# A decoder layer's cross-attention: VectorE turns the maxima, row transfers in four pieces, two loads merged, two sums moved

## Chip, core and metric

The kernel runs on one NeuronCore of one Trainium2 chip. Times are device microseconds (us) of that core. The median of three runs of the kernel before is 801.43 us (801.19 to 803.54).

## The reference

```python
x = x + attn(layernorm(x))             # 32 heads of 16, causal, grouped keys; x is (4, 512, 512)
x = x + xattn(layernorm(x), ctx, ctx)  # ctx (4, 512, 512) is both keys and values
x = x + ffn(layernorm(x))              # three ternary-weight matmuls, activations rounded to 8 bits

def xattn(q, k, v):                    # (b, 512, 512) each, 8 heads of 64 rows: 32 heads in all
    qk = einsum('bdm,bdn->bmn', qh, kh) * 64 ** -0.5
    sm = softmax(qk, axis=-1)
    return einsum('bmn,bcn->bcm', sm, vh)

def ffn(x):                            # qlinear rounds x per row: scale = max|x| / 127 + eps
    return qlinear(silu(qlinear(x, w_gate)) * qlinear(x, w_up), w_down)
```

The scores of the cross-attention decide a sharp softmax, so the kernel computes them from a high and a low part of queries and keys.

## The kernel before

All engines run programs written out by hand and meet through semaphores. The function `rest_of_layer` holds the part that the change touches: attention output (steps 0 to 18), cross-attention (steps `i` of `attend_context`, 3 to 43) and feed-forward bodies (`feed(i)`). The last eight steps of the cross-attention, 36 to 43, alternate with feed-forward bodies 2 to 9.

The 32 heads are taken as 16 pairs, one head on partitions 0 to 63 and one on 64 to 127. `pair_due(i, k)` says which pair has a piece of work in step `i`, `k` steps after its first; each piece comes every second step. For pair p, in order of time:

- **First scores** (L1597): steps 2p+1 and 2p+2, four 128x512 blocks each, into the banks `p1`, three in turn. VectorE takes each block's maximum over 512 queries' scores into a column of `mx` (L1408).
- **Turn**: at the end of step 2p+2 TensorE transposes `mx` (128x8) into a `p1` bank (L1603), and VectorE copies it negated into `mrow` (8x128, L1414). The turn takes a place in the rotation of the `p1` banks.
- **Rows**: SyncE moves `mrow` in two transfers, one a head, to partition 0 and partition 64 of `mrows` (L1043), at the start of its step 2p+3.
- **Second scores** (L1631): steps 2p+4 and 2p+5. Four terms a block: high by high, low by high, high by low, and `unit` by `mrows`, which subtracts the maxima. All waits for the pair's inputs stand before the first term. ScalarE takes the exponential (L1276).
- **Sums**: GpSimd adds the halves of the exponentials (L1174, L1179), VectorE too (L1438), TensorE sums over partitions with a matrix of ones in step 2p+8 (L1659), ScalarE copies the sums to `den` (L1301) and sends eight partitions of them from its own queue (L1288), VectorE takes reciprocals (L1445, step 2p+10), SyncE stores them to memory (L1097, step 2p+11) and loads them back, each head's row repeated on 64 partitions, in two transfers into `rden` (L1105, step 2p+12).
- **Weighing**: TensorE multiplies exponentials by values `vt` (L1644, steps 2p+5 and 2p+6). Values are loaded in two transfers of 128 KB (L1092).
- **Result**: VectorE multiplies by `rden` (L1457, at the end of step 2p+13, after that step's four maxima) and GpSimd adds to the tokens (L1183).

The pair's keys are split by ScalarE (L1245) and VectorE (L1420). Pairs 14 and 15 sum into a bank of their own, in steps 36 and 38, ahead of the other work of these steps; step 38 stands ahead of feed-forward body 4. Each engine works strictly in the order of its own list, and so does each queue of transfers: what an instruction waits for holds up all that follows on its engine.

Of the kernel before, what the change touches and what calls it, by code (L numbers as in the profile page):

```python
# [6 lines left out]
F32 = mybir.dt.float32  # L7
F32R = mybir.dt.float32r
# [882 lines left out]
def rest_of_layer(nc, io, scr, keep, out):  # L891
# [10 lines left out]
    with ExitStack() as ctx:  # L902
# [18 lines left out]
        halves = m.sb("halves", [P, 2, DIM]); total = m.sb("total", [P, UNROLL, DIM])  # L921
        mx = m.sb("mx", [P, 2, 2 * KD]); mrow = m.sb("mrow", [2 * KD, 2, P], F32R)
        den = m.sb("den", [P, DIM]); few = m.sb("few", [2 * RUNS, 2, H]); inv = m.sb("inv", [2 * RUNS, 2, H])
# [31 lines left out]
        p1_full, p1_used = m.sem("p1_full"), m.sem("p1_used")  # L955
        scores, p2_used, halved, summed, weighted = (m.sem(s) for s in ("scores", "p2_used", "halved", "summed", "weighted"))
        first_total, second_total = m.sem("first_total"), m.sem("second_total")
        few_in, inv_done, inv_out, rden_in = (m.sem(s) for s in ("few_in", "inv_done", "inv_out", "rden_in"))
# [36 lines left out]
        for i in range(1, D_LAST):  # L995
            for n in range(STEP):
                if 0 <= i - 1 < HEADS_X:
                    p1_use["f", i, n] = len(p1_use)
            if i >= 2 and i % 2 == 0 and (i - 2) // 2 < PAIRS:
                p1_use["turn", (i - 2) // 2] = len(p1_use)  # L1000
            for n in range(STEP):
                if 0 <= i - 4 < HEADS_X:
                    p2_use["s", i - 4, n] = len(p2_use)
            if i >= 8 and i % 2 == 0 and (i - 8) // 2 < PAIRS:
                p2_use["sum", (i - 8) // 2] = len(p2_use)
        P1_USES, P2_USES = len(p1_use), p2_use["s", HEADS_X - 1, STEP - 1] + 1
        LATE_SUMS = PAIRS - 2

# [12 lines left out]
        def _(sp):  # L1021
# [14 lines left out]
            def load_maxima(p):  # L1036
                sp.wait_ge(p1_used, p1_use["turn", p] + 1)
                if p == 0:
                    sp.wait_ge(padded, 2)
                if due(STEP * 2 * (p - 1)):  # L1040
                    sp.wait_ge(scores, STEP * 2 * (p - 1))
                for a in range(2):
                    sp.dma_start(mrows[a * H:a * H + 1, p % 2, :].bitcast(F32), mrow[a * KD:(a + 1) * KD, p % 2, :].bitcast(F32)).then_inc(m_in[p % 2], 16)  # L1043

# [28 lines left out]
            def attend_context(i):  # L1073
                p = pair_due(i, 3)
                if p is not None:
                    load_maxima(p)
                p = pair_due(i, -1)
                if p is not None and p >= 3:
                    sp.wait_ge(kl_done, p - 1)
                    load_context_rows(p)  # L1080
                p = pair_due(i, -2)
                if p is not None and p >= 3:
                    load_query_rows(p)
                p = pair_due(i, 1)
                if p is not None and p >= 2:
                    load_query_low(p)
                p = pair_due(i, 3)
                if p is not None:
                    if due(p - 1):
                        sp.wait_ge(weighted, p - 1)  # L1090
                    for a in range(2):
                        sp.dma_start(vt[:, 2 * (p % 2) + a, :, :], io["ctx_t"][bass.ds(2 * p + a, 1)].rearrange("o (k p) c -> p (o k) c", p=P)  # L1092
                                     ).then_inc(vt_in[p % 2], 16)
                p = pair_due(i, 11)
                if p is not None:
                    sp.wait_ge(inv_done, p + 1)
                    sp.dma_start(scr["inv"][2 * RUNS * p:2 * RUNS * (p + 1), :], inv[:, p % 2, :]).then_inc(inv_out, 16)  # L1097
                p = pair_due(i, 12)
                if p is not None:
                    sp.wait_ge(inv_out, 16 * (p + 1))  # L1100
                    if due(p):
                        sp.wait_ge(y_done, p)
                    for a in range(2):
                        at = RUNS * (2 * p + a)
                        sp.dma_start(rden[a * H:(a + 1) * H, :], scr["inv"][at:at + RUNS, :].rearrange("r c -> (r c)")  # L1105
                                     .unsqueeze(0).broadcast_to([H, DIM])).then_inc(rden_in, 16)

# [21 lines left out]
        def _(pool):  # L1129
            nc.gpsimd.memset(mrows[:].bitcast(F32), 0.0)  # L1130
            nc.gpsimd.memset(unit[:].bitcast(F32), 0.0).then_inc(padded, 1)
            pool.wait_ge(padded, 1)
            nc.gpsimd.memset(unit[0:1, :].bitcast(F32), 1.0)
            nc.gpsimd.memset(unit[H:H + 1, :].bitcast(F32), 1.0).then_inc(padded, 1)
            pool.wait_ge(padded, 2)
# [86 lines left out]
        def _(act):  # L1222
# [34 lines left out]
            def attend_context(i):  # L1257
# [38 lines left out]
                p = pair_due(i, 8)  # L1296
                if p is not None:
                    act.wait_ge(summed, p + 1)
                    if due(p):
                        act.wait_ge(few_in, 32 * p)  # L1300
                    nc.scalar.activation(den[:], p2_bank("sum", p)[:], ACT.Copy).then_inc(p2_used, 1)  # L1301

# [8 lines left out]
            def feed(i):  # L1311
# [36 lines left out]
                keep_turned_products(0)  # L1348
                gate(2)
                quantised(i - 1)  # L1350
                keep_turned_products(1)
# [24 lines left out]
        def _(dve):  # L1376
# [26 lines left out]
            def maximum(i, n):  # L1403
                if not 0 <= i - 1 < HEADS_X:
                    return
                p, a, blk = unit_of(i - 1, n)
                dve.wait_ge(p1_full, p1_use["f", i, n] + 1)
                nc.vector.reduce_max(mx[:, p % 2, KD * a + blk:KD * a + blk + 1], p1_bank("f", i, n)[:], AX.X).then_inc(p1_used, 1)  # L1408

            def keep_maxima(p):  # L1410
                dve.wait_ge(p1_full, p1_use["turn", p] + 1)
                if p >= 2:
                    dve.wait_ge(m_in[p % 2], 32 * (p // 2))
                nc.vector.tensor_scalar(mrow[:, p % 2, :], p1_bank("turn", p)[0:2 * KD, 0:P], -1.0, None, ALU.mult).then_inc(p1_used, 1)  # L1414

# [6 lines left out]
            def early(c):  # L1422
# [5 lines left out]
                if c == TURN_AT:  # L1428
                    keep_maxima(0)

            def attend_context(i):
# [19 lines left out]
                if p is not None and p >= 1:  # L1451
                    keep_maxima(p)
                p = pair_due(i, 13)
                if p is not None:
                    dve.wait_ge(rden_in, 32 * (p + 1))
                    dve.wait_ge(y_kept, p + 1)
                    nc.vector.tensor_tensor(y[:, p % UNROLL, :], y[:, p % UNROLL, :], rden[:], ALU.mult).then_inc(y_done, 1)  # L1457
# [105 lines left out]
        def _(pe):  # L1563
# [35 lines left out]

            def turn_maxima(p):  # L1600
                use = p1_use["turn", p]
                pe.wait_ge(p1_used, use)
                nc.tensor.transpose(p1_bank("turn", p)[0:2 * KD, 0:P], mx[:, p % 2, :], keep["ident"][:]).then_inc(p1_full, 1)  # L1603

            def early(c):
                if c in BLOCKS_AT:
                    first_scores(*BLOCKS_AT[c])
                if c == TURN_AT:
                    turn_maxima(0)

            def second_scores(j, b):
# [4 lines left out]
                if b == 0 and j % 2 == 0:  # L1616
# [4 lines left out]
                    pe.wait_ge(ql_in[p % LSLOTS], 16 * (p // LSLOTS + 1))  # L1621
                    pe.wait_ge(m_in[p % 2], 32 * (p // 2 + 1))
                for term, (left, right) in enumerate(((kh[:, p % UNROLL, :], qh[:, p % QSLOTS, :]), (kl[:, p % 2, :], qh[:, p % QSLOTS, :]),
                                                      (kh[:, p % UNROLL, :], ql[:, p % LSLOTS, :]), (unit, mrows[:, p % 2, :]))):
                    for a in range(2):
                        use = p2_use["s", j, 2 * b + a]
                        if term == 0 and due(use - SBANKS + 1):
                            pe.wait_ge(p2_used, use - SBANKS + 1)
                        rows = slice(a * H, (a + 1) * H)
                        weights = unit[rows, :] if term == 3 else left[rows, blk * P:(blk + 1) * P]  # L1630
# [4 lines left out]
            def weigh(p, nb):  # L1635
                if nb == 0:
                    if due(p):
                        pe.wait_ge(y_kept, p)
                    else:
                        pe.wait_ge(C["x1"], TILES)  # L1640
                    pe.wait_ge(vt_in[p % 2], 32 * (p // 2 + 1))
                pe.wait_ge(p2_used, p2_use["s", 2 * p + nb // 2, 2 * (nb % 2) + 1] + 1)
# [19 lines left out]
            def attend_context(i):  # L1662
# [3 lines left out]
                p = pair_due(i, 8)  # L1666
                if p is not None:
                    sum_probs(p)
# [5 lines left out]
                if p is not None:  # L1674
                    weigh(p, 2)
                    weigh(p, 3)
                p = pair_due(i, 2)
                if p is not None and p >= 1:
                    turn_maxima(p)

            def feed(i):
# [53 lines left out]
                if j == HELD + 2:  # L1735
                    down(HELD + 1, KF // 2, KF // 2)
                gate_up(2)
                turn_products(j, 1)
                gate_up(3)
# [102 lines left out]
```

## Time and profile before

| | |
|---|---|
| median of 3 runs | 801.43 us |
| profiled execution | 804.03 us, span 801.88 us |
| TensorE matmul busy | 769.0 us, 96% |
| VectorE busy | 639.2 us, 80% |
| ScalarE busy | 491.6 us, 61% |
| GpSimd busy | 423.4 us, 53% |
| turns on TensorE (L1603) | 16, from 435.6 to 588.9 us |
| granted TensorE clock, mean | 0.987 |

In the profile PE is TensorE's matmuls and PEld its weight loads, DVE is VectorE, ACT is ScalarE, POOL is GpSimd, SPq and ACTq are the transfers issued by SyncE and ScalarE. A bracket behind a row is the idle time of the engine just before it and what ended that. L numbers are lines of the kernel. A matmul in float32 appears as two instructions, and the duration of a matmul is longer than the distance to the next one, since they overlap.

### The profile page before, as it was taken

To read this page: it belongs to the slowest core of one execution; us is meant where nothing else is said; L and a number is where in the kernel's file an instruction comes from. 1 tells how busy PE (TensorE), PEld (TensorE's weight loads), DVE (VectorE), ACT (ScalarE), POOL (GpSimd) and SP (SyncE) were. 2 spreads that over 40 slices of the span, in tenths; PEclk is the share of its full clock that TensorE was granted. 3 is DMA by queue.
4 is the path that set the end of the run, shared out by engine and by line. 5 is a ranking of instruction groups with operands and counts; after the bars stand their busy time and mean duration, and the time that the engine had idled before them with its cause. 6 is when DMAs were issued, how large, how long until landed. Compare 5 with 4: busy or idle time off the path is not lost.

```text
span 801.9 us, 15448 instructions
## 1 busy us (share of the span) xinstructions
PE 769.0 (96%) x4902; PEld 423.2 (53%) x4902; DVE 639.2 (80%) x1905; ACT 491.6 (61%) x844; POOL 423.4 (53%) x458
## 2 busy tenths in 40 slices
PE   7999999999999999998998999999998899999997
PEld 6777544444444444444875555555543455555543
DVE  7676888889888888971689678888876798888883
ACT  4665467667767767765465455555556565576564
POOL 5554479999999600000334367777785344423321
PEclk9999999999999999999999899999999999999999
DMA  8898665445445212201485534444420011000001
GB/s 290 303 380 290 197 163 138 130 128 142 131 118 148 70 52 64 63 3 53 154 289 193 170 96 130 126 125 120 119 72 11 13 41 40 18 24 27 27 19 47
DMA packets 65760, 94.79 MB, mean 118 GB/s; under 512 B 26928, under 2 KB 38448, under 8 KB 64144
## 3 DMA queue, kind: packets, MB, share of 16 engines
q1 hardware_dynamic: 61216, 80.77, 31.8%
q0 software_dynamic: 3952, 12.98, 6.0%
q8 instruction: 39, 0.64, 0.3%
q14 instruction: 41, 0.34, 0.1%
q10 hardware_dynamic: 512, 0.07, 0.1%
HBM read 72.88 MB, written 20.51 MB: 116 GB/s over the span
## 4 chain that ended last, share of the span: by engine, by line
PE 32%; DVE 11%; issue 4%; ACT 2%; POOL 1%; DMA 1%; SPq 1%; ACTq 0%; DVEq 0%; POOLq 0%
PE r_p L1697 12%; PE r_p L1631 4%; PE r_pn L1644 4%; PE r_p L1727 3%; PE r_pn L1727 3%; DVE r_mx L1408 3%; DVE r_kl L1420 3%; PE r_p L1597 2%; PE r_p L1711 2%; DVE r_stats L1378 1%; DVE r_total L1438 1%; DVE tok L1397 1%; DVE r_inv L1445 1%; PE r_p L1579 1%; DVE r_xl L1391 1%
## 5 line engine op out<-in xcount | busy, mean ns | idle before, releaser
L787 ACT ACTIVATE b_probs<-ab_j 128x512 f32<-128x512 f32 (+1 forms) x352 | 177.1, 560 | 26.7 <-PE ab_j L852 15.8
L148 DVE CUSTOM_DVE_ANT_0 b_junk<-ab_t,mask_qk 128x128 bf16<-128x128 f32 (+2 forms) x243 | 108.8, 486 | 26.9 <-PE ab_t L128 26.8
L852 PE MATMUL ab_j<-qs,ks 98*128 98x512 bf16 (+1 forms) x352 | 123.3, 365 | 1.6 <-DVE a_rest L533 0.8
L1276 ACT ACTIVATE r_probs<-r_p 128x512 f32<-128x512 f32 x128 | 69.5, 599 | 72.3 <-PE r_p L1631 71.0
L148 DVE CUSTOM_DVE_ANT_0 b_junk<-ab_e,mask_qk 128x256 bf16<-128x256 f32 (+2 forms) x237 | 103.7, 482 | 1.8 <-PE ab_e L128 1.5
L1408 DVE TENSOR_REDUCE r_mx<-r_p 128x1 f32<-128x512 f32 x128 | 82.4, 675 | 23.9 <-PE r_p L1597 22.0
L1174 POOL TENSOR_TENSOR r_halves<-r_probs 128x1024 f32<-128x1024 f32 x32 | 77.3, 2414 | 38.5 <-DVE r_total L1438 26.9
L1323 ACT ACTIVATE r_silu<-r_p,r_cg 128x512 f32<-128x512 f32 x64 | 44.3, 692 | 51.4 <-PE r_p L1697 50.2
L870 PE MATMUL ab_pv<-b_probs,v 128*32 128x512 f32 (+3 forms) x1024 | 75.6, 436 | 0.0
L1201 POOL TENSOR_SCALAR r_h<-r_h,r_fh 128x1024 f32<-128x1024 f32 x32 | 37.9, 1198 | 64.1 <-DVE r_fh L1538 64.1
L128 PE MATMUL ab_e<-ks,qs 96*128 96x128 bf16 (+3 forms) x269 | 64.9, 304 | 4.1 <-DVE mx L148 0.9
L1697 PE MATMUL r_p<-wg,r_zt 128*128 128x512 bf16 x256 | 65.7, 379 | 1.4 <-ACT r_zt L1361 1.4
L1697 PE MATMUL r_p<-wu,r_zt 128*128 128x512 bf16 x256 | 65.7, 379 | 0.0
L1644 PE MATMUL r_pn<-r_probs,r_vt 128*64 128x512 f32 x256 | 61.3, 599 | 0.5 <-ACT r_y L1255 0.5
L1492 DVE TENSOR_TENSOR r_h<-r_p,r_silu 128x512 f32<-128x512 f32 x64 | 44.1, 689 | 22.1 <-PE r_p L1697 16.6
L128 PE MATMUL ab_t<-ks,qs 96*128 96x128 bf16 (+2 forms) x243 | 59.0, 304 | 2.3 <-DVE mx L148 0.2
L870 PEld LDWEIGHTS ab_pv<-b_probs,v 128*32 128x32 f32 x1024 | 30.0, 109 | 48.3 <-issue 41.6
L1130 POOL MEMSET r_mrows<- 128x1024 f32 x1 | 1.0, 952 | 102.6 <-POOLq L238 102.6
L797 ACT ACTIVATE b_osb<-ab_pv 128x512 f32<-128x512 f32 x32 | 19.1, 597 | 58.2 <-PE ab_pv L870 58.2
L855 PE MATMUL ab_j<-mask_kq,identb 128*128 128x512 bf16 x128 | 49.3, 385 | 0.0
L852 PEld LDWEIGHTS ab_j<-qs,ks 98*128 98x128 bf16 x352 | 34.5, 98 | 25.5 <-ACT b_probs L787 10.4
L1500 DVE TENSOR_REDUCE r_hpart<-r_h 128x1 f32<-128x512 f32 x64 | 43.9, 686 | 2.2
(178 smaller groups left out, 1749.9 us busy)
## 6 DMA issues: line engine op xcount, KB each, us to landing
qs<-q_parts SPq DMA_DIRECT2D x32, 192.0 KB, 3.4
q_parts<-a_parts SPq DMA_DIRECT2D x15, 384.0 KB, 6.1
a_wst<-in_w_gate SPq DMA_DIRECT2D x4, 1024.0 KB, 7.5
a_wst<-in_w_up SPq DMA_DIRECT2D x4, 1024.0 KB, 9.9
a_wst<-in_w_down SPq DMA_DIRECT2D x4, 1024.0 KB, 8.4
qs<-q_parts SPq DMA_DIRECT2D x32, 128.0 KB, 3.3
b_wst<-in_w_gate POOLq DMA_DIRECT2D x16, 256.0 KB, 4.0
b_wst<-in_w_up POOLq DMA_DIRECT2D x16, 256.0 KB, 3.1
```

The lines of the kernel that those rows point to most:

```text
L128: last = nc.tensor.matmul(st.bank(keep, i, k)[:, c:c + w], keep["qs"][0:STACK, s, j, qt * P:(qt + 1) * P], keep["ks"][0:STACK, s, 0:w], st ...
L148: best = nc.vector.tensor_tensor_reduce(out=junk[:, 2 * (st.use[i, k] % slots) + n, 0:w], in0=bank[:, c:c + w], in1=keep["mask_qk"][:, SEQ ...
L787: nc.scalar.activation(pblock(j % 2, kb)[:, j0:j0 + nj, c:c + w], p2[(NE * j + n) % BANKS2][:, 0:nj * w].rearrange("p (j c) -> p j c", j=n ...
L852: last = nc.tensor.matmul(bank, ks[0:STACK + 2, s, kb * P:(kb + 1) * P], qs[0:STACK + 2, s, j0:j0 + nj, kb * P + c:kb * P + c + w], start= ...
L855: last = nc.tensor.matmul(bank, keep["identb"][:], keep["mask_kq"][:].rearrange("p j c -> p (j c)"), start=False, stop=True)
L870: last = nc.tensor.matmul(pv[2 * HDIM * j:2 * HDIM * (j + 1), kb * P:], v, pblock(j3 % 2, kb)[:, j, :], start=kb == 0, stop=kb == TPB - 1, ...
L1174: nc.gpsimd.tensor_tensor(halves[:], probs[:, slot, 0:2, :], probs[:, slot, 2:4, :], ALU.add).then_inc(halved, 1)
L1276: nc.scalar.activation(probs[:, 2 * (p % 2) + a, blk, :], p2_bank("s", j, n)[:], ACT.Exp, scale=SCALE).then_inc(p2_used, 1)
L1408: nc.vector.reduce_max(mx[:, p % 2, KD * a + blk:KD * a + blk + 1], p1_bank("f", i, n)[:], AX.X).then_inc(p1_used, 1)
L1644: last = nc.tensor.matmul(pn[a * H:(a + 1) * H, :], vt[:, 2 * (p % 2) + a, nb, :], probs[:, 2 * (p % 2) + a, nb, :], start=nb == 0, stop=n ...
L1697: last = nc.tensor.matmul(bank[g % len(bank)][:], zt[:, j % 2, k, :], keep[w][:, k, n * 512:(n + 1) * 512], start=k == 0, stop=k == KD - 1)
L1727: last = nc.tensor.matmul(pf[j % 2][:], ht[j % 2][:, k, :], keep["wd"][:, k, :], start=k == 0, stop=k == KF - 1)
```

## The change

- VectorE itself turns the maxima. `mx` is widened to 128x32, zeroed once by GpSimd; a transpose in blocks of 32x32 writes `mt`, so that the eight rows of each block of 32 partitions lie on partitions 32g to 32g+7. The TensorE turn, its place in the `p1` banks and the copy to `mrow` go; `unit` holds -1 instead of a negated row.
- The rows go to `mrows` in four transfers, one a block, each of eight pieces of 32 numbers.
- TensorE's wait for the rows moves to the fourth term of a pair's first block.
- The values of a pair come in one transfer, and so do its inverse sums.
- The sum of pair 14 moves behind the weighing of step 36; that of pair 15, with ScalarE's copy, behind the third gate product of feed-forward body 4.

```diff
-        mx = m.sb("mx", [P, 2, 2 * KD]); mrow = m.sb("mrow", [2 * KD, 2, P], F32R)
+        mx = m.sb("mx", [P, 2, H // 2]); mt = m.sb("mt", [P, 2, H // 2])
...
-            if i >= 2 and i % 2 == 0 and (i - 2) // 2 < PAIRS:
-                p1_use["turn", (i - 2) // 2] = len(p1_use)
...
             def load_maxima(p):
-                sp.wait_ge(p1_used, p1_use["turn", p] + 1)
+                sp.wait_ge(mt_done, p + 1)
...
-                for a in range(2):
-                    sp.dma_start(mrows[a * H:a * H + 1, p % 2, :].bitcast(F32), mrow[a * KD:(a + 1) * KD, p % 2, :].bitcast(F32)).then_inc(m_in[p % 2], 16)
+                rows = mrows[0:H + 1:H, p % 2, :].bitcast(F32).rearrange("a (k g c) -> a k g c", k=KD, g=KD)
+                for g in range(KD):
+                    at = g * P // KD
+                    sp.dma_start(rows[:, :, g, :], mt[at:at + 2 * KD, p % 2, :]).then_inc(m_in[p % 2], 16)
...
-                    for a in range(2):
-                        sp.dma_start(vt[:, 2 * (p % 2) + a, :, :], io["ctx_t"][bass.ds(2 * p + a, 1)].rearrange("o (k p) c -> p (o k) c", p=P)
-                                     ).then_inc(vt_in[p % 2], 16)
+                    sp.dma_start(vt[:, 2 * (p % 2):2 * (p % 2) + 2, :, :], io["ctx_t"][bass.ds(2 * p, 2)].rearrange("o (k p) c -> p o k c", p=P)
+                                 ).then_inc(vt_in[p % 2], 16)
...
-                    for a in range(2):
-                        at = RUNS * (2 * p + a)
-                        sp.dma_start(rden[a * H:(a + 1) * H, :], scr["inv"][at:at + RUNS, :].rearrange("r c -> (r c)")
-                                     .unsqueeze(0).broadcast_to([H, DIM])).then_inc(rden_in, 16)
+                    sp.dma_start(rden[:], scr["inv"][2 * RUNS * p:2 * RUNS * (p + 1), :].rearrange("(a r) c -> a (r c)", a=2)
+                                 .unsqueeze(1).broadcast_to([2, H, DIM])).then_inc(rden_in, 16)
...
+            nc.gpsimd.memset(mx[:], 0.0)
...
-            nc.gpsimd.memset(unit[0:1, :].bitcast(F32), 1.0)
-            nc.gpsimd.memset(unit[H:H + 1, :].bitcast(F32), 1.0).then_inc(padded, 1)
+            nc.gpsimd.memset(unit[0:1, :].bitcast(F32), -1.0)
+            nc.gpsimd.memset(unit[H:H + 1, :].bitcast(F32), -1.0).then_inc(padded, 1)
...
-            def keep_maxima(p):
-                dve.wait_ge(p1_full, p1_use["turn", p] + 1)
+            def turn_maxima(p):
+                dve.wait_ge(p1_used, STEP * 2 * (p + 1))
                 if p >= 2:
-                    dve.wait_ge(m_in[p % 2], 32 * (p // 2))
-                nc.vector.tensor_scalar(mrow[:, p % 2, :], p1_bank("turn", p)[0:2 * KD, 0:P], -1.0, None, ALU.mult).then_inc(p1_used, 1)
+                    dve.wait_ge(m_in[p % 2], 64 * (p // 2))
+                nc.vector.transpose(mt[:, p % 2, :], mx[:, p % 2, :]).then_inc(mt_done, 1)
...
-                    pe.wait_ge(m_in[p % 2], 32 * (p // 2 + 1))
...
+                        if term == 3 and a == 0 and b == 0 and j % 2 == 0:
+                            pe.wait_ge(m_in[p % 2], 64 * (p // 2 + 1))
...
                 p = pair_due(i, 8)
-                if p is not None:
+                if p is not None and p < LATE_SUMS:
                     sum_probs(p)
...
-                p = pair_due(i, 2)
-                if p is not None and p >= 1:
-                    turn_maxima(p)
+                if i == 2 * LATE_SUMS + 8:
+                    sum_probs(LATE_SUMS)
...
                 gate_up(2)
+                if i == LAST_SUM_BODY:
+                    sum_probs(PAIRS - 1)
                 turn_products(j, 1)
```

ScalarE's `keep_sums(PAIRS - 1)` likewise stands behind `gate(2)` of that body.

## Rows read from the trace of the kernel before

**Rows 1.** Windows: busy us of PE, PEld, DVE, ACT, POOL; clock; DMA share; GB/s.
```profile
500.00:540.00 40.00, 39.51 (x242) 21.34 (x240) 32.48 (x51) 22.05 (x43) 30.55 (x16) 1.00 0.42 128
```

**Rows 2.** Chain of waits, middle of the cross-attention: start, us, what.
```profile
514.36 1.48 DVE r_kl L1420
...
524.61 1.48 DVE r_kl L1420
```

**Rows 3.** Timeline of TensorE, one pair: start, duration, line, operation, tiles.
```profile
519.33 1.94 PE L1644 MATMUL r_pn<-r_probs,r_vt 128*64 128x512 f32 x8
521.19 0.50 PE L1597 MATMUL r_p<-r_kh,r_qh 64*128 64x512 f32 x2
...
522.23 0.40 PE L1631 MATMUL r_p<-r_mrows,r_unit 64*128 64x512 f32 x2
...
524.73 1.89 PE L1644 MATMUL r_pn<-r_probs,r_vt 128*64 128x512 f32 x8
...
526.95 0.50 PE L1597 MATMUL r_p<-r_kh,r_qh 64*128 64x512 f32 x2
```

**Rows 4.** Timeline of VectorE, the same pair.
```profile
516.80 0.28 DVE L1414 TENSOR_SCALAR r_mrow<-r_p 8x128 fp32r<-8x128 f32 x1 [0.37 <-PE r_p L1603]
...
519.62 0.68 DVE L1457 TENSOR_TENSOR r_y<-r_y,r_rden 128x512 f32<-128x512 f32 x1
521.73 0.69 DVE L1408 TENSOR_REDUCE r_mx<-r_p 128x1 f32<-128x512 f32 x1 [1.42 <-PE r_p L1597]
...
526.01 0.68 DVE L1408 TENSOR_REDUCE r_mx<-r_p 128x1 f32<-128x512 f32 x1
```

**Rows 5.** Timeline of all engines at the seam into the cross-attention.
```profile
434.74 0.18 DVE L1381 BATCH_NORM_AGGREGATE r_mv<-r_stats 128x2 f32<-128x6 f32 x1
...
445.78 0.27 PE L1603 MATMUL r_p<-ident,r_mx 128*8 128x128 f32 x1 [0.33 <-DVE r_mx L1408]
```

**Rows 6.** Chain of waits at the seam.
```profile
438.70 2.49 DMA r_mrows<-r_mrow
```

**Rows 7.** Timeline of SyncE's transfers, one pair: start and duration of the issue.
```profile
517.10 1.30 SPq L1043 DMA_DIRECT2D r_mrows<-r_mrow  x2
...
519.58 0.98 SPq L1092 DMA_DIRECT2D r_vt<-in_ctx_t  x2
520.61 0.50 SPq L1097 DMA_DIRECT2D inverse_sums<-r_inv  x1
...
523.67 1.15 SPq L1105 DMA_DIRECT2D r_rden<-inverse_sums  x2
```

**Rows 8.** DMA issues, page part 6: count, KB each, median us to landing.
```profile
r_rden<-inverse_sums SPq DMA_DIRECT2D x32, 128.0 KB, 2.8
...
r_mrows<-r_mrow SPq DMA_DIRECT2D x32, 2.0 KB
r_few<-r_den ACTq DMA_DIRECT2D x32, 2.0 KB
```

**Rows 9.** Windows: the inverse sums' load; the busiest stretch of the seam.
```profile
524.50:527.00 2.50, 2.37 (x13) 0.57 (x9) 2.19 (x3) 1.30 (x3) 2.42 (x2) 1.00 0.29 105
441.00:445.00 4.00, 3.67 (x18) 3.04 (x18) 2.88 (x5) 1.51 (x3) 0.00 (x0) 0.50 1.02 317
```

**Rows 10.** DMA view of 524.5 to 527: busy tenths in 40 slices.
```profile
DMA  0000000225255354427586456354240110000000
```

**Rows 11.** Page part 2: GB/s in 40 slices of the span.
```profile
GB/s 290 303 380 290 197 163 138 130 128 142 131 118 148 70 52 64 63 3 53 154 289 193 170 96 130 126 125 120 119 72 11 13 41 40 18 24 27 27 19 47
```

**Rows 12.** Timeline near step 36: GpSimd's addition and VectorE's total.
```profile
602.36 1.27 POOL L1183 TENSOR_TENSOR tok<-r_y,tok 128x512 f32<-128x512 f32 x1
602.43 1.75 DVE L1438 TENSOR_TENSOR r_total<-r_halves 128x512 f32<-128x512 f32 x1 [2.92 <-POOL r_halves L1174]
```

**Rows 13.** Timeline of TensorE at the sums of pairs 13 and 15.
```profile
595.39 1.08 PE L1659 MATMUL r_p<-r_total,ones 128*64 128x512 f32 x4
...
630.59 1.08 PE L1659 MATMUL r_p<-r_total,ones 128*64 128x512 f32 x4 [2.54 <-issue]
```

More of the change, by code:

```diff
@@ L956, in rest_of_layer @@
         scores, p2_used, halved, summed, weighted = (m.sem(s) for s in ("scores", "p2_used", "halved", "summed", "weighted"))
+        mt_done = m.sem("mt_done")
         first_total, second_total = m.sem("first_total"), m.sem("second_total")
@@ L1006, in rest_of_layer @@
         P1_USES, P2_USES = len(p1_use), p2_use["s", HEADS_X - 1, STEP - 1] + 1
-        LATE_SUMS = PAIRS - 2
+        LATE_SUMS, LAST_SUM_BODY = PAIRS - 2, E_FIRST + 2
         def p1_bank(*key):
@@ L1296, in attend_context, with keep_sums @@
                 p = pair_due(i, 8)
-                if p is not None:
[L1298 to L1301, printed above, removed]
+                if p is not None and p < PAIRS - 1:
+                    keep_sums(p)
+            def keep_sums(p):
+                act.wait_ge(summed, p + 1)
+                if due(p):
+                    act.wait_ge(few_in, 32 * p)
+                nc.scalar.activation(den[:], p2_bank("sum", p)[:], ACT.Copy).then_inc(p2_used, 1)
             def quantised(j):
@@ L1349, in feed @@
                 gate(2)
+                if i == LAST_SUM_BODY:
+                    keep_sums(PAIRS - 1)
                 quantised(i - 1)
@@ L1406, in maximum @@
                 p, a, blk = unit_of(i - 1, n)
+                if p1_use["f", i, n] == 0:
+                    dve.wait_ge(padded, 1)
                 dve.wait_ge(p1_full, p1_use["f", i, n] + 1)
                 nc.vector.reduce_max(mx[:, p % 2, KD * a + blk:KD * a + blk + 1], p1_bank("f", i, n)[:], AX.X).then_inc(p1_used, 1)
-            def keep_maxima(p):
-                dve.wait_ge(p1_full, p1_use["turn", p] + 1)
+            def turn_maxima(p):
+                dve.wait_ge(p1_used, STEP * 2 * (p + 1))
                 if p >= 2:
-                    dve.wait_ge(m_in[p % 2], 32 * (p // 2))
-                nc.vector.tensor_scalar(mrow[:, p % 2, :], p1_bank("turn", p)[0:2 * KD, 0:P], -1.0, None, ALU.mult).then_inc(p1_used, 1)
+                    dve.wait_ge(m_in[p % 2], 64 * (p // 2))
+                nc.vector.transpose(mt[:, p % 2, :], mx[:, p % 2, :]).then_inc(mt_done, 1)
             def keys_low(p):
@@ L1428, in early @@
                 if c == TURN_AT:
-                    keep_maxima(0)
+                    turn_maxima(0)
             def attend_context(i):
@@ L1451, in attend_context @@
                 if p is not None and p >= 1:
-                    keep_maxima(p)
+                    turn_maxima(p)
                 p = pair_due(i, 13)
                 if p is not None:
-                    dve.wait_ge(rden_in, 32 * (p + 1))
+                    dve.wait_ge(rden_in, 16 * (p + 1))
                     dve.wait_ge(y_kept, p + 1)
@@ L1598, in first_scores @@
                                      start=True, stop=True).then_inc(p1_full, 1)
[L1600 to L1603, printed above, removed]
             def early(c):
@@ L1607, in early @@
                     first_scores(*BLOCKS_AT[c])
-                if c == TURN_AT:
-                    turn_maxima(0)
             def second_scores(j, b):
@@ L1640, in weigh @@
                         pe.wait_ge(C["x1"], TILES)
-                    pe.wait_ge(vt_in[p % 2], 32 * (p // 2 + 1))
+                    pe.wait_ge(vt_in[p % 2], 16 * (p // 2 + 1))
                 pe.wait_ge(p2_used, p2_use["s", 2 * p + nb // 2, 2 * (nb % 2) + 1] + 1)
@@ L1666, in attend_context @@
                 p = pair_due(i, 8)
-                if p is not None:
+                if p is not None and p < LATE_SUMS:
                     sum_probs(p)
@@ L1737, in feed @@
                 gate_up(2)
+                if i == LAST_SUM_BODY:
+                    sum_probs(PAIRS - 1)
                 turn_products(j, 1)
```

## The prediction

> **What bounds the kernel now.** I read the windows first, then the chain of waits, then one pair of heads on each engine, and last the DMA issues. TensorE is busy 39.51 of 40 us in the middle of the cross-attention [rows 1]; only at its two ends does it stand, before a sum and at the seam [rows 5, 13]. The chain of a pair runs through VectorE as well: its pieces alternate between TensorE's matmuls and VectorE's maxima and key remainder [rows 2]. A pair takes 10.25 us there (514.36 to 524.61), and 10.26 from one turn to the next. On TensorE eight weighing matmuls without a turn behind them take 1.86 us to the next first score (519.33 to 521.19); with a turn 2.22 us (524.73 to 526.95) [rows 3]. So a turn costs 0.36 us, and TensorE without it needs 9.90 us a pair. VectorE idles 1.42 us a pair before the first maximum of the even step, and 0.37 us for the turn [rows 4].
>
> **The change, part by part.**
>
> Turn on VectorE. The TensorE transpose goes (0.36 us a pair), and so does VectorE's copy of 0.28 us behind its wait of 0.37 us. In comes a VectorE transpose of 128x32. No row shows one: the copy of 8x128 at 0.28 us [rows 4] bounds it above, an operation on 128x6 at 0.18 [rows 5] below; I take 0.2, nearer to the second, which has few columns on all partitions too. It starts after the last maximum (526.01 + 0.68 + 0.03 = 526.72) and ends at 526.92, while the next first score, now starting at 526.59, is full about 0.54 us later (521.19 to 521.73), at 527.13. It is hidden, with 0.2 us to spare; each 0.1 us beyond costs that much a pair. The first turns have no late neighbour. At the seam TensorE loses a wait for the copied row, but the rows' landing ends that stretch anyway (2.49 us after its issue) [rows 6]: two more issues before it, against a wait now behind three terms, leave a gain near 0.2. Turn 1 stood 0.33 us idle and 0.2 busy [rows 5], 0.55 gained. Turn 2 gains 0.2, turns 3 to 5 0.36 each: 2.05 us in all until then. The zeroing of the maxima and the new wait on it lie long before first use.
>
> Rows in four pieces. Two issues took 1.30 us [rows 7], so four take 2.65. The last is issued 2 us after the turn and lands at most 2.49 us later [rows 6], at 4.5. TensorE's first use is now the fourth term of the even step: 1.04 us after its first score (521.19 to 522.23) [rows 3], which is 4.5 us (an odd step) behind 526.59, so 5.2 us after the turn. So this fits, by 0.7 us. Behind the four issues on SyncE stand the key rows, low queries, values, the store of the inverse sums, query rows and the load of the inverse sums: all 1.3 us later. The values' single issue gives 0.49 us back (half of 0.98). The store then starts 3.51 + 1.34 - 0.49 = 4.35 us after the turn and the load 3.06 us after that (520.61 to 523.67) [rows 7], at 7.4.
>
> Values in one transfer. Its outer dimension stays the 128 partitions; it is needed some 9 us after its issue. Nothing.
>
> Inverse sums in one transfer. This decides the case. The old load has 64 destination partitions outermost, the new one a source whose slowest dimension is the pair's two heads. The page prints a landing time for every DMA group but two, the rows (outer dimension 4) and the sums to few partitions (outer 8) [rows 8]. I read this as transfers that finish on fewer than 16 engines, so that the full set of completions is never seen, and expect the new load on two engines. The Trainium skill says so outright ("DMA: Bandwidth & Descriptors", "Why a DMA increments its semaphore by 16 and not by 1"): the largest number up to 16 that divides the slowest dimension of both sides; the two missing times agree with it, and no row shows a transfer on two engines with a time.
> Price: 262 KB (105 GB/s over 2.5 us) took 0.29 of 16 engines [rows 9], 11.6 engine-us, on two engines 5.8 us. Below it stands the best slice of the page, 380 GB/s or 23.8 an engine [rows 11], 5.5 us; above it 317 GB/s with the engines full [rows 9], 19.8 an engine, 6.6 us. The old load's first issue is at 523.67 [rows 7] and its data begin in the eighth of 40 slices, at 524.94 [rows 10], 1.3 us later; its second, issued near 524.25, lands 2.8 us after [rows 8], at 527.05, 0.35 after the last busy slice. So 1.3 + 5.8 + 0.35 = 7.45 us instead of 2.8. Ends: 1.3 + 5.5 + 0.35 = 7.15, and, with all dead time before the data, 2.8 - 0.36 + 5.8 = 8.25.
>
> It is waited for on VectorE, in the multiplication of y after the odd step's four maxima; queued behind it are the next even step's maxima and its turn. This closes a loop over two pairs: turn, 7.4 to the load's issue, 7.45 to its landing, 0.60 for y, 4.28 from the first to the last maximum of the even step (521.73 to 526.01) [rows 4], 0.68 + 0.03 + 0.2 for the last maximum and the turn. That is 20.65. One more term: GpSimd adds y into the tokens right behind the multiplication, and VectorE's total now falls upon it. Such a collision stands in the trace: GpSimd ends at 603.63, VectorE's total of 0.68 us lasts until 604.18, 0.55 after it [rows 12]. In the loop the addition would end 2.05 us after y's start and the total 2.6 instead of 1.88: +0.7. The loop is 21.3 us against 2 x 10.26 = 20.52 now and 19.8 if all were hidden. Multiplications begin in step 13, so five loops are passed up to the last turn: 5 x 0.78 = +3.9 us. The moments of the second token tile (0.92 us) now lie in the loop, while those of the first, which cost 0.67, go under: +0.25.
> At the last turn: -2.05 + 3.9 + 0.25 = +2.1 us.
>
> The tail. Turn 15 ends 10.8 us after turn 14 (9.9 and the moments' 0.9), so the load of pair 10 lands 14.85 - 10.8 = 4.05 us after turn 15, where y now starts at once. VectorE then has y (0.68), the scaling of the first tokens behind GpSimd's addition (until about 6.4) and 1.3 us of small operations before the total of pair 13, which ends at 8.4. TensorE wants it 6.0 us after the turn (595.39 against 589.4) [rows 13]: 2.4 us of stall. The reordered sum of pair 14 and what VectorE's later idle time gives I put at 0.5 back: +1.9 us (bounds 0 and 4).
> The last sum. TensorE idles 2.54 us before it [rows 13]; moved behind the third gate product, it meets a finished total. Its own 0.9 us stays, and ScalarE's copy of 0.60 us now stands before a token copy and a gate: 0.2 lost. -2.3 us.
>
> **Sum.** +2.1 + 1.9 - 2.3 = +1.7 us. The profiled execution took 804.03 us (span 801.88 and 2.15 around it), 2.6 above the median of 801.43. So 805.7 for such an execution, and 803.1 against the median. For two engines alone the ends 7.15 and 8.25 move five loops and the tail by -0.3 and +0.8 each, 801 to 808; with the tail's bounds 799 to 810, of which I take 800 to 808 as its own range.
>
> **Rivals.**
> All 16 engines take the load (the outer two split further, or moved inside). Then nothing waits, the turn's 0.36 is saved ten more times (3.6), the tail keeps 0.3, the last sum 2.3: 2.05 + 3.6 + 0.3 + 2.3 = 8.2, so 793.2 us. For it: VectorE's and the rows' slack above. Against it: the two missing landing times.
> Slower: the load takes over 7.7 us, as when it runs at the 19.8 GB/s an engine of the full stretch at 441 us [rows 9]: 6.6 us of data and the longer dead time of 2.44 make 9.05, each loop 1.6 more, and the tail 1: about 812. It decides from a load of 7.6 us (803.8); at 8.25 the time is 808. For it: every piece reads the same two rows of memory. Against it: little else moves on the two engines then.
> Rows late: if an issue in pieces of 128 bytes cost 0.9 us instead of 0.65, the slack of 0.7 us would go, and TensorE would stand at the fourth term; with the load spread well that makes 793 into 795 to 800. The issues of 4 and of 8 pieces cost the same, which speaks against it.
> The change not doing what it says: the turn surely leaves TensorE.
>
> **Chances.** Two engines near my forecast (799.0 to 803.8) 0.40; two engines beyond 803.8, the slow rival in it, 0.32; sixteen engines 0.20, and rows late, mostly still faster, 0.05; two engines below 799 0.03. No change within 0.3% (799.0 to 803.8, about what a measurement tells) is 0.40, slower 0.34, faster 0.26. The range has both signs: 793 to 808; the forecast's own is 800 to 808.
>
> **What would show it.** No landing time printed for the load, or one of 7 to 8 us; VectorE's multiplication idle on that DMA for some us in nearly every pair; pair periods of about 10.6 against 10.26 (9.9 if I am wrong); the total lasting over 1 us where it was 0.68; the transpose at 0.2 us; no idle at TensorE before its fourth term; 2.5 us less idle near 628. A landing of 3 us overturns the forecast towards 793.

## The result

The changed kernel takes 804.71 us (median of 20 runs, 801.9 to 808.05), the kernel before in the same series 802.0 us (20 runs, 799.29 to 803.74). The ratio is 1.0037, 95% interval 1.0025 to 1.0048: by the ratio 3.0 us slower, by the two medians 2.7. The forecast was +1.7 us and 803.1 us. The time lies in its range of 800 to 808 us, but just outside what it called no change (up to 803.8 us, chance 0.40): it is the outcome "slower", to which it gave 0.34.

### The profile page after: what moved, and what is told of

Read it like the earlier page. It is cut to its first block, busy times and chain, and to the rows that moved or that the text cites. A ratio compares the mean times of both kernels' runs of the same rounds, so it can differ in the third digit from the quotient of the medians.

```text
span 803.1 us, 15349 instructions
## 1 busy us (share of the span) xinstructions
PE 763.3 (95%) x4832; PEld 417.2 (52%) x4886; DVE 639.9 (80%) x1905; ACT 491.1 (61%) x844; POOL 422.4 (53%) x459
## 4 chain that ended last, share of the span: by engine, by line
PE 26%; DVE 9%; DMA 9%; issue 4%; SPq 3%; ACT 2%; POOL 1%; ACTq 0%; DVEq 0%; POOLq 0%
PE r_p L1696 12%; DMA r_rden<-inverse_sums 6%; PE r_p L1726 3%; PE r_pn L1726 3%; DMA inverse_sums<-r_inv 3%; DVE r_mx L1414 2%; PE r_p L1710 2%; PE r_p L1631 2%; SPq L1044 2%; PE r_pn L1644 2%; DVE r_kl L1426 1%; DVE r_stats L1382 1%; DVE tok L1401 1%; PE r_p L1603 1%; SPq L1033 1%
## 5 line engine op out<-in xcount | busy, mean ns | idle before, releaser
L1696 PE MATMUL r_p<-wg,r_zt 128*128 128x512 bf16 x245 | 63.5, 379 | 2.1 <-ACT r_zt L1365 1.4
L128 PEld LDWEIGHTS ab_e<-ks,qs 96*128 96x128 bf16 x269 | 23.0, 98 | 39.6 <-DVE mx L148 14.5
```

Source lines behind the costliest of these rows:

```text
L128: last = nc.tensor.matmul(st.bank(keep, i, k)[:, c:c + w], keep["qs"][0:STACK, s, j, qt * P:(qt + 1) * P], keep["ks"][0:STACK, s, 0:w], st ...
L1696: last = nc.tensor.matmul(bank[g % len(bank)][:], zt[:, j % 2, k, :], keep[w][:, k, n * 512:(n + 1) * 512], start=k == 0, stop=k == KD - 1)
```

## The profile after

The profiled execution took 804.89 us, its span 803.1 us at a mean granted clock of 0.994. Of the page, the busy times and the chain of work that ended last:

```profile
PE 763.3 (95%) x4832; PEld 417.2 (52%) x4886; DVE 639.9 (80%) x1905; ACT 491.1 (61%) x844; POOL 422.4 (53%) x459
...
PE 26%; DVE 9%; DMA 9%; issue 4%; SPq 3%; ACT 2%; POOL 1%; ACTq 0%; DVEq 0%; POOLq 0%
```

The waits (instruction, what it waited for, us in total, times, longest us):

```profile
DVE r_y L1463 <- DMA r_rden<-inverse_sums: 28.1, 11, 4.5
PEld r_p L1631 <- DMA r_mrows<-r_mt: 12.1, 9, 2.8
PE r_p L1631 <- DMA r_mrows<-r_mt: 8.5, 6, 2.4
```

PEld and PE wait side by side for the rows, so their times are not to be added up. In the trace of before VectorE waited once, 1.1 us, for the inverse sums, and TensorE once, 0.8 us, for the rows. Now VectorE waits eleven times in 16 pairs for the load, and TensorE up to nine times for the rows. The DMA issues (KB of one, then median us to landing, where one is found):

```profile
r_vt<-in_ctx_t SPq DMA_DIRECT2D x16, 256.0 KB, 4.0
r_rden<-inverse_sums SPq DMA_DIRECT2D x16, 256.0 KB
r_mrows<-r_mt SPq DMA_DIRECT2D x64, 1.0 KB
inverse_sums<-r_inv SPq DMA_DIRECT2D x16, 4.0 KB, 3.6
```

Against [rows 8] the inverse sums have lost their landing time, as forecast. One pair on VectorE, which answers to [rows 4]:

```profile
517.17 1.31 DVE L1444 TENSOR_TENSOR r_total<-r_halves 128x512 f32<-128x512 f32 x1
...
521.47 0.68 DVE L1414 TENSOR_REDUCE r_mx<-r_p 128x1 f32<-128x512 f32 x1
522.18 0.21 DVE L1420 STREAM_TRANSPOSE r_mt<-r_mx 128x32 f32<-128x32 f32 x1
522.32 2.44 DVE L1414 TENSOR_REDUCE r_mx<-r_p 128x1 f32<-128x512 f32 x4
528.68 0.69 DVE L1463 TENSOR_TENSOR r_y<-r_y,r_rden 128x512 f32<-128x512 f32 x1 [3.93 <-DMA r_rden<-inverse_sums]
```

The turn is 0.21 us and no engine waits for it. The four maxima of the odd step are through by 524.76; then VectorE stands 3.93 us for a load that SyncE had issued at 520.47. SyncE's queue over the same pair (answers to [rows 7]), and TensorE at its fourth term:

```profile
520.47 0.52 SPq L1103 DMA_DIRECT2D r_rden<-inverse_sums  x1
522.42 2.33 SPq L1044 DMA_DIRECT2D r_mrows<-r_mt  x4
524.80 0.67 SPq L1022 DMA_DIRECT2D r_k<-in_ctx  x1
...
526.47 0.58 SPq L1097 DMA_DIRECT2D inverse_sums<-r_inv  x1
527.15 0.40 SPq L1028 DMA_DIRECT2D r_qh<-x_normed_high  x1
531.50 0.52 SPq L1103 DMA_DIRECT2D r_rden<-inverse_sums  x1
```
```profile
529.62 0.50 PE L1631 MATMUL r_p<-r_mrows,r_unit 64*128 64x512 f32 x2 [2.19 <-DMA r_mrows<-r_mt]
```

What the load does in between is seen in windows of 1 us (columns: stretch, its length, busy us of PE, PEld, DVE, ACT, POOL, then the granted clock, the mean busy share of 16 DMA engines, GB/s):

```profile
523.00:524.00 1.00, 1.00 (x9) 0.85 (x9) 1.00 (x2) 0.92 (x2) 1.00 (x1) 1.00 0.13 51
524.00:525.00 1.00, 1.00 (x7) 0.34 (x7) 0.76 (x2) 0.55 (x2) 1.00 (x1) 1.00 0.14 53
525.00:526.00 1.00, 1.00 (x8) 0.15 (x3) 0.00 (x0) 1.00 (x3) 0.16 (x1) 1.00 0.14 53
526.00:527.00 1.00, 1.00 (x8) 0.68 (x8) 0.00 (x0) 0.03 (x1) 0.00 (x0) 1.00 0.68 150
```

Two engines of 16 are a share of 0.125, and for three microseconds the share stands at 0.13 to 0.14. I read this as two engines running full while fourteen do next to nothing; a mean over 16 doesn't show that by itself, the experiments below bear it out. 262 KB at some 52 GB/s are 5.0 us.

Where the time went, by stretches of the profiled executions (us):

| kernel | zeroing of `mrows` to turn 0 | turn 0 to 15 | to first token turn of feed-forward | to first output store | to last store |
|---|---|---|---|---|---|
| before | 61.7 | 151.5 | 13.8 | 40.0 | 156.3 |
| before, sums moved | 59.1 | 151.5 | 13.9 | 37.0 | 156.2 |
| before, merged load | 59.1 | 156.0 | 14.3 | 41.3 | 156.4 |
| after | 59.1 | 158.0 | 15.5 | 37.0 | 156.2 |
| after, two loads | 59.1 | 144.5 | 13.7 | 37.1 | 156.1 |

The first column of the first row is no difference between the kernels. A window of before's profile shows a lower granted clock there, and with 1.00 in that place the others all have 59.1:

```profile
376.00:385.00 9.00, 7.99 (x29) 6.29 (x30) 2.61 (x4) 1.68 (x3) 1.49 (x4) 0.62 0.34 117
```

Without it the changed kernel loses 6.5 us up to the last turn and 1.7 behind it, and gains 3.0 at the sums: +5.1 us by profiles, +3.0 by the ratio of the runs. The 2 us between them lie in the profiled execution of before, which is no typical one: without the dip (2.6 us), and without the 1.2 us by which it reached the zeroing later (at 376.0 us, the changed kernel at 374.8), it is 1.8 us under its median of 802.0. Why, is open.

## The experiments

Theory: the merged load runs on two DMA engines, the largest number up to 16 that divides its slowest dimension (the outermost one, here the pair's two heads), and closes a loop over two pairs. Rivals: one issue, its place in the queue, or its source of two rows is what costs; or the rows or the values cost. A ratio below is to the kernel before, measured in the same series, with its 95% interval; where medians of two series are compared, up to 0.9 us of the difference can be the series'.

**Inverse sums in two transfers again.**

```diff
-  sp.dma_start(rden[:], ... "(a r) c -> a (r c)", a=2).unsqueeze(1).broadcast_to([2, H, DIM]))
+  for a in range(2):   # one head each
+      sp.dma_start(rden[a * H:(a + 1) * H, :], ....unsqueeze(0).broadcast_to([H, DIM]))
```

> The changed kernel with the inverse sums loaded in two transfers again, one a head, the rest as changed. Theory (the merged load runs on two engines): its landing time is printed again at about 2.8 us, VectorE's multiplication and TensorE's fourth term wait for nothing, pairs take 9.9 us, and the time falls to 793 us, 11 us under the changed kernel (ratio to before 0.989 to 0.991). Rival (the four row transfers or SyncE's later queue are what costs): it stays within 2 us of the changed kernel, ratio 1.001 to 1.004, and TensorE still waits for the rows.

Measured: 789.06 us, ratio to before 0.9853 [0.9827, 0.9878]. This kernel beats both, and by 4 us what was expected of it (793). The turns come every 9.83 us, VectorE waits 3.2 us in all for the load (two times), TensorE once for the rows, 0.8 us at the weight load. The total no longer meets GpSimd's addition, and the load's data take about 2 us:

```profile
518.32 0.21 DVE L1422 STREAM_TRANSPOSE r_mt<-r_mx 128x32 f32<-128x32 f32 x1
518.66 2.48 DVE L1416 TENSOR_REDUCE r_mx<-r_p 128x1 f32<-128x512 f32 x4
521.06 0.79 DVE L1465 TENSOR_TENSOR r_y<-r_y,r_rden 128x512 f32<-128x512 f32 x1
523.16 0.69 DVE L1416 TENSOR_REDUCE r_mx<-r_p 128x1 f32<-128x512 f32 x1 [1.31 <-PE r_p L1605]
523.76 0.68 DVE L1446 TENSOR_TENSOR r_total<-r_halves 128x512 f32<-128x512 f32 x1
```
```profile
518.00:519.00 1.00, 1.00 (x10) 0.74 (x10) 0.83 (x3) 0.00 (x0) 0.92 (x2) 1.00 0.56 123
519.00:520.00 1.00, 1.00 (x12) 0.90 (x10) 1.00 (x3) 0.41 (x1) 1.00 (x1) 1.00 0.39 140
520.00:521.00 1.00, 1.00 (x10) 0.59 (x8) 1.00 (x2) 0.67 (x2) 1.00 (x1) 1.00 0.01 2
```

So the merged load costs some 15 us here (15.6 by the medians, 14.8 by the ratios), and all the rest of the change gains 11.8 by the ratio.

**The merged load alone**, in the kernel before (the diff above turned round).

> The kernel before with one edit: the inverse sums in one transfer. Theory (two engines): slower, though nothing else is changed; a loop of two pairs is 0.8 us shorter on SyncE than in the changed kernel and 0.2 longer at the turn, so 20.7 us against 20.5, and with the tail 2 to 5 us slower than before (ratio 1.003 to 1.006); VectorE's multiplication waits for the load in most pairs. Rival (one transfer costs no more than two): within 0.1%, and SyncE has 0.6 us a pair more to spare.

Measured: 806.7 us, ratio 1.0058 [1.0039, 1.0077], 4.7 us slower. No landing time is printed for it, and the load takes 7.1 to 8.2 us to VectorE's multiplication:

```profile
DVE r_y L1455 <- DMA r_rden<-inverse_sums: 16.8, 11, 4.1
```

The same load costs 4.7 us with the turn on TensorE and some 15 with it on VectorE: the loop takes 20.9 to 22.4 us (21.5 in the mean, expected 20.7) where it would be 20.5, and 21.2 to 24.0 in the changed kernel where it would be 19.7 (in the two loops that hold a token tile's moments, 21.2 and 20.4).

**Two transfers, each of both heads and half the columns.** As many issues and bytes as the two of one head, but a slowest dimension of 2.

```diff
-  for a in range(2): ... .broadcast_to([H, DIM])
+  for n in range(2):   # cols: half of DIM
+      sp.dma_start(rden[:, cols], ... "(a r) c -> a (r c)", a=2)[:, cols].unsqueeze(1).broadcast_to([2, H, DIM // 2]))
```

> The changed kernel with the inverse sums in two transfers, but each for both heads and half of the columns: the slowest dimension of the source is still two. Theory (number of engines counts, not number of transfers): no landing time printed, the waits stay, the time is that of the changed kernel or 1 to 3 us more, for pieces of 1 KB (ratio to before 1.003 to 1.008). Rival (one large transfer is slow because it is one): as with a transfer a head, ratio 0.990.

Measured: 815.59 us, ratio 1.0171 [1.0145, 1.0198]: the number of issues is not it. It is some 11 us slower than the changed kernel, where 1 to 3 were expected: 8.7 to 9.5 us pass from issue to multiplication. The pieces of 1 KB, where one transfer has 2 KB, are the likely reason; no run changes them alone.

```profile
DVE r_y L1465 <- DMA r_rden<-inverse_sums: 39.2, 12, 5.3
```

**The load on ScalarE's queue**, merged, behind the fourth exponential, out of SyncE's order. SyncE's store of the inverse sums takes over a wait for an earlier multiplication.

```diff
-  sp.wait_ge(inv_out, 16 * (p + 1)) ... sp.dma_start(rden[:], ...)
+  act.wait_ge(inv_out[p % 2], 16 * (p // 2 + 1)) ... act.dma_start(rden[:], ...)
```

> The changed kernel with its merged load issued from ScalarE's queue, behind the last exponential of the even step, instead of SyncE's. Theory (two engines move the bytes, whoever asks): the landing stays 7 to 8 us after the issue, VectorE's multiplication still waits in most pairs, and the time is within 4 us of the changed kernel (ratio to before 1.000 to 1.009); the rows no longer stand behind it in one queue, so TensorE's wait for them (8.5 us in all) may fall. Rival (it is the order in SyncE's queue that costs): the waits go and the ratio is 0.99 or less.

Measured: 808.34 us, ratio 1.0072 [1.005, 1.0093]. VectorE waits 32.8 us in 12 times, and TensorE still 9.7 us for the rows. The place in SyncE's order of issues isn't it either.

**One head a transfer, split 62 + 2 rows, and split 60 + 4 rows.** This takes the two-row source away. Both kernels have four issues, sources of one row, 2 KB pieces and the same bytes; only the split differs.

```diff
-  sp.dma_start(rden[a * H:(a + 1) * H, :], ...)
+  for lo, hi in ((0, 62), (62, H)):      # in the other kernel 60
+      sp.dma_start(rden[a * H + lo:a * H + hi, :], ....broadcast_to([hi - lo, DIM]))
```

> The changed kernel with the inverse sums loaded head by head, each head in two transfers of 62 and 2 rows (four issues a pair; the source of each is one row of memory). Theory (the number of DMA engines is the largest up to 16 that divides the slowest dimension): 62 rows go to two engines, 127 KB a head, so the data of a head take 2.9 us alone; if both heads fall on the same two engines the load lands some 7 to 8 us after its issue as the merged one did, VectorE's multiplication waits on it in most pairs, and the time is 803 to 812 us; on two engines each it is near 4.6 us and the time 790 to 798. No landing time is printed for the 62-row transfers. Rival (what made the merged load slow is its source of two rows, or the single issue, not the slowest dimension): as the kernel with 60 rows, within 0.3%.

> The same with 60 and 4 rows a transfer. Theory: 60 rows go to 15 engines, 4 rows (8 KB) to four; the load lands in about 3 us, the multiplication waits little, and what is left against the kernel with one transfer a head (789.1 us) is SyncE's time for two more issues a pair, some 1.0 us in a loop that had little to spare: 789 to 795 us, clearly below the kernel with 62 rows. Rival: same time as with 62 rows, since the bytes, pieces and issues are the same.

Measured: 62 rows 807.38 us, ratio 1.0077 [1.0045, 1.0109]; 60 rows 790.3 us, ratio 0.9847 [0.9819, 0.9875]. Two rows moved from one transfer to the next make 17 us by the medians, 18 by the ratios. The waits with 62 rows:

```profile
DVE r_y L1466 <- DMA r_rden<-inverse_sums: 30.9, 12, 4.6
PEld r_p L1634 <- DMA r_mrows<-r_mt: 12.9, 11, 2.6
PE r_p L1634 <- DMA r_mrows<-r_mt: 8.2, 10, 2.2
```

and with 60, where TensorE waits for the rows in one place only, 0.8 us, as with two loads:

```profile
DVE r_y L1466 <- DMA r_rden<-inverse_sums: 4.0, 4, 2.1
```

The windows behind an issue (at 521.09 with 62 rows, 520.70 with 60) show the same level of two engines, and its absence:

```profile
526.00:527.00 1.00, 1.00 (x5) 0.34 (x6) 0.54 (x1) 0.83 (x2) 0.93 (x1) 1.00 0.14 51
527.00:528.00 1.00, 1.00 (x6) 0.14 (x2) 0.00 (x0) 0.75 (x2) 0.00 (x0) 1.00 0.15 53
```
```profile
522.00:523.00 1.00, 1.00 (x10) 0.70 (x6) 1.00 (x3) 0.97 (x2) 1.00 (x1) 1.00 0.53 186
523.00:524.00 1.00, 1.00 (x7) 0.37 (x8) 0.58 (x2) 0.64 (x2) 0.58 (x1) 1.00 0.07 20
```

Both heads' 62-row transfers share the same two engines: from 522 to 528 us the share never stands at four of 16 (0.25), and the multiplication comes 7.9 to 8.7 us after the first issue, not near the 4.6 that were estimated for two pairs of engines. The Trainium skill ("DMA: Bandwidth & Descriptors", "Why a DMA increments its semaphore by 16 and not by 1") says that such transfers go to the lowest-numbered engines; the shares agree, though they don't show the numbers. No landing time is printed for the 60-row transfers either: on fifteen engines, by the rule. Two more issues a pair cost the kernel with 60 rows nothing that can be told from the one with two loads.

**The last two sums moved, alone**, in the kernel before.

```diff
+  if i == 2 * LATE_SUMS + 8: sum_probs(LATE_SUMS)        # step 36, behind the weighing
+  if i == LAST_SUM_BODY: sum_probs(PAIRS - 1)            # behind gate_up(2); keep_sums behind gate(2)
```

> The kernel before with one edit: the last two sums moved as in the change. Theory: the 2.54 us of TensorE's idle time before the last sum goes, and 0.2 comes back elsewhere: 2.3 to 2.7 us faster, ratio 0.997. Rival (the late sum holds up ScalarE's gates and VectorE's products in its new place): within 1 us of before.

Measured: 799.33 us, ratio 0.9963 [0.9948, 0.9978]: 3.0 us gained by the ratio (2.4 by the medians), 3.0 in the table of stretches.

**The turn without the moved sums**: two loads, sums in their old places.

```diff
-  if i == LAST_SUM_BODY: sum_probs(PAIRS - 1)   # and keep_sums, and the line for LATE_SUMS
```

> The changed kernel with the inverse sums in two transfers and the last two sums in their old places: what the turn, the rows and the values bring alone. With both effects independent: the stretch from the first to the last turn stays 144.4 us as in the run with two loads, and about 3.0 us more pass between the first token turn and the first store: 2.5 to 3 us slower than that run, 9 us under before, ratio 0.988. Rival (part of the gain of the moved sums came only because the turns were faster, or the reverse): it differs from 0.9853 / 0.9963 = 0.989 by more than 0.3%.

Measured: 796.18 us, ratio 0.9931 [0.9907, 0.9956]: against 0.9853 that is 6.3 us more than with the sums moved (7.1 by the medians of two series), not 3. Faster turns leave less time ahead of the old places, as I read it. TensorE idles 1.44 us before the sum of pair 14, where it was 0.84, and ScalarE stands longer for the last one; the fourth stretch is 42.2 us, not 40.0:

```profile
593.55 1.08 PE L1659 MATMUL r_p<-r_total,ones 128*64 128x512 f32 x4 [1.44 <-issue]
...
619.86 1.71 PE L1659 MATMUL r_p<-r_total,ones 128*64 128x512 f32 x4 [2.55 <-issue]
```
```profile
621.61 0.60 ACT L1305 ACTIVATE r_den<-r_p 128x512 f32<-128x512 f32 x1 [7.11 <-PE r_p L1659]
```

The profiled executions are 5.3 us apart (794.56 and 789.27), and 5.1 of them lie in this stretch. TensorE's idle time before the sum of pair 14 makes 1.4 of these and that before the last one 2.5; the remaining 1.1 are not placed.

**Rows awaited before the first term, and values in two transfers**, with two loads of the sums.

```diff
+  pe.wait_ge(m_in[p % 2], 64 * (p // 2 + 1))    # ahead of the terms, not at term 3
-  sp.dma_start(vt[:, 2 * (p % 2):2 * (p % 2) + 2, :, :], ...)
+  for a in range(2): sp.dma_start(vt[:, 2 * (p % 2) + a, :, :], ...)
```

> The run with two loads, with two small parts of the change undone: TensorE waits for the rows ahead of the first term again, and the values come in two transfers. Theory (with the load out of their way the rows land 4 us after the turn, 1 us before the first term): no wait for the rows, pairs stay at 9.83 us, ratio to before 0.985 to 0.987. Rival (the later wait is what makes four issues bearable): TensorE waits for the rows in every pair, 0.3 us or more, ratio 0.990 and above.

Measured: 790.72 us, ratio 0.9862 [0.9842, 0.9882], against 0.9853 [0.9827, 0.9878] for the two loads alone. By the medians neither part is worth anything that can be told once the load lands in time. The profile shows one place, the first period, from turn 0 to turn 1: 8.12 us, where the run with two loads has 6.79. TensorE waits 0.9 us there ahead of the first term.

**The second token tile's moments a step later**, with two loads, an attempt to go below.

```diff
-  if i == 24:
+  if i == 25:
```

> The run with two loads, with the moments of the first token tile moved from the end of step 24 to the end of step 25, where VectorE idles 1.3 us before its next maximum. Expected: the one pair of 10.5 us becomes 9.85, 0.6 us faster than the run with two loads, too little to be told from it for sure (ratio to before 0.983 to 0.986). If the moments cost as much there, nothing changes.

Measured: 790.0 us, ratio 0.9852 [0.9826, 0.9877]: no difference from 0.9853. The profile shows the one long pair gone (turn 0 to 15 in 143.4 us, not 144.5), the medians don't.

## Why the prediction was right, and where it was not

**The deciding step held.** Two engines: shown by the share of 0.13 to 0.14 and by 62 against 60 rows. The Trainium skill's rule ("DMA: Bandwidth & Descriptors", "Why a DMA increments its semaphore by 16 and not by 1") gives two engines for 62 and fifteen for 60, and the two runs agree, 807.38 and 790.3 us. The landing, put at 7.45 with ends 7.15 and 8.25, came at 7.06 to 8.21 from issue to multiplication, 7.5 in the mean.

**The loop held in form; one term was too small.** In the ten loops of the trace:

| us | turn to store | store to load | load to multiplication | to the turn after next | loop |
|---|---|---|---|---|---|
| forecast | 4.35 | 3.06 | 7.45 | 6.5 | 21.3 |
| after | 3.9 to 5.4 | 3.2 to 5.4, mean 4.2 | 7.1 to 8.2 | 6.3 to 6.9 | 21.2 to 24.0, mean 22.6 |
| two loads | 4.3 to 5.4 | 3.1 to 5.2 | 3.7 to 4.8 | 7.1 | 19.7 to 20.4 |

The mis-sized term is "the load 3.06 us after that". That came from one store of before; in the changed kernel it is 4.2 in the mean of ten loops and up to 5.4. The two engines are one part of why. The three stores issued 1.9 to 2.5 us before a merged load landed took 4.8 to 5.4 us to land, such as that of 526.47, and the key rows issued at 524.80 took 5.0; but one store issued just as a load landed, that of 538.87, took 5.3 too. The kernel before with the merged load alone shows it most plainly: its store of 604.47, issued 1.0 us behind a merged load, landed 6.8 us after its issue, and that of 595.89 took 6.0; in the kernel before the same two took 2.7 (at 604.66) and 2.5, though the latter was issued 1.2 us behind a load as well. The stores of 604.47 and 604.66, KB and us to landing:

```profile
inverse_sums<-r_inv SPq DMA_DIRECT2D x1, 4.0 KB, 6.8
inverse_sums<-r_inv SPq DMA_DIRECT2D x1, 4.0 KB, 2.7
```

A transfer over all engines seems to have a part on the two full ones and to wait for them; the rows show the delay, not the engines. I had priced the slow load for its own reader, and not for what shares its engines. The other part is not the slow load's: with two loads the same distance is 3.7 us in the mean, so that of the 1.1 us above 3.06 only some 0.4 go with the merged load. Most stores of that kernel land in 3.4 to 3.7 us instead of 3.0, and one takes 5.1; which transfers do that is open (the median is 3.5, and 3.2 with the values in two).

**The gain before the loop was too small, its price too.** Turn 0 to 5: 48.4 us before, 45.1 after, 3.3 gained where 1.85 was put (the seam's 0.2 apart, of which nothing is seen). The surplus lies in the first two periods, 8.42 and 9.19 us before, 6.78 and 8.16 after, 2.7 gained for 0.75. The prediction left TensorE's clock out of it. At this seam the granted clock is 0.50, the lower level of 1.2 GHz, from 438.4 to 445.2 us before and only from 435.6 to 439.0 after, each time behind some 2 us in which TensorE hardly worked (before, then after):

```profile
439.00:443.00 4.00, 3.23 (x11) 2.07 (x12) 3.71 (x7) 1.45 (x2) 0.19 (x1) 0.50 0.62 184
439.00:443.00 4.00, 3.94 (x31) 2.71 (x29) 3.96 (x8) 3.32 (x8) 0.00 (x0) 1.00 0.85 297
```

With two loads and the rows awaited before the first term the clock is at 0.50 from 434.1 to 440.9 and the first period is back at 8.12. So the later wait, or the single transfer of the values that is undone in the same run, is worth 1.3 us once, at the seam. What shortened the second period is open.

Turn 5 to 15: 103.2 before, 112.9 after, 9.7 lost where 4.15 was put. These ten periods are five loops: five times 21.3 and the 0.9 of the moments would be 107.4, so a loop came out 1.1 us longer than put, nearly all of it from the store's term. The turn, with the rows and the values, was worth 0.43 us a pair (10.26 to 9.83) instead of 0.36.

**The rows did not fit.** "Fits by 0.7" rested on a landing of 2.49 us. The issues cost less than was said (2.33 us for 2.65), but the rows of 522.42 served TensorE only at 529.62, 7.4 us after the turn. With 60 rows a transfer and in the kernel with two loads that wait is one of 0.8 us at the seam, so there the rows fit; with 62 it is back. It goes with the slow load: small transfers behind a full pair of engines. The rows' own destination, partitions 0 and 64 of `mrows`, also has two as its slowest dimension, so by the same rule they use just that pair; no run changes that dimension. TensorE's wait didn't lengthen the loop, since VectorE's multiplication held the maxima up at the same time and its distance to the turn after next stayed at 6.3 us; this is read from the trace, no run separates it.

**The collision held.** In seven of the ten loops the total took 1.31 to 1.40 us, as put; it took 1.07 once and 0.68 in the two loops where the multiplication waited less than 0.7 us, as in all with two loads.

**The tail's number held, its place did not:** 15.5 against 13.8 us, +1.7 where +1.9 was put. But 2.4 us of stall were put at the sum of pair 13, less 0.5, and nothing at the rows; measured are 0.49 us at that sum and 1.31 at the last rows, the same delay as above. That the two add up to the forecast is luck:

```profile
597.88 0.49 PE L1631 MATMUL r_p<-r_mrows,r_unit 64*128 64x512 f32 x2 [1.31 <-DMA r_mrows<-r_mt]
599.79 1.08 PE L1659 MATMUL r_p<-r_total,ones 128*64 128x512 f32 x4 [0.49 <-DVE r_total L1444]
```

**The last sum** was put at -2.3; both moved sums give -3.0, of 2.54 and 0.84 us of idle time. That they interact with the turn was not forecast, though the changed kernel itself gains no more than these 3.0.

**The total** was close, +1.7 against +3.0, because a gain and a loss were both undersized: -1.85 for -3.3, and +4.15 for +9.7. The nearness of 803.1 to 804.71 is part luck. Of the rivals, sixteen engines is what the kernel with two loads does: put at 793.2, it takes 789.06, 4 us less for the same reasons.

## What to carry to other kernels

Before merging two transfers, look at the slowest dimension of both sides: a broadcast source with its two groups outermost ran as if on two engines, and 62 rows were as bad as 2, where 60 rows were as good as 64. Other counts were not tried. A DMA whose landing time the page lacks, and a DMA share that stands near 2/16 while nothing else moves, were the signs here. Price such a transfer twice, for its own reader and for all that is issued until it lands, and against the loop as fast as the rest of the change makes it, not as it was.

## What was not expected of the hardware

- The merged load ran at 51 to 53 GB/s, some 26 an engine if all of it went over two, above the 23.8 of the page's best slice in [rows 11].
- Full-width transfers issued while it ran (524.8 to 527.2 us) landed in 4.7 to 5.3 us, where the medians of these groups in the kernel with two loads are 3.2 to 3.8. That kernel too has one such burst, of 4.9 to 5.4 us (530.6 to 533.2), which no slow load explains.
- A store of 4 KB issued 1.0 us behind a merged load landed after 6.8 us, where it takes 2.7 without one.
- Two transfers of 62 rows behaved as if they took the same two engines, while the share left fourteen idle.
- A transpose of 128x32 in float32 on VectorE takes 0.21 us.
